# Moving the fourth score wave, the value products and a magnitude within the loop of the first attention

## The reference

```python
# x: 8 batches x 100 tokens x 256, context: 8 x 361 x 192, 16 heads of 16
q = (x @ Wq + bq).reshape(B, N, 16, 16)
k = (y @ Wk + bk).reshape(B, M, 16, 16)
v = (y @ Wv + bv).reshape(B, M, 16, 16)
attn = softmax(einsum('bnhd,bmhd->bhnm', q, k) / 4)
out = einsum('bhnm,bmhd->bnhd', attn, v).reshape(B, N, 256)
h = relu(out @ W1 + b1);  result = h @ W2 + b2
# beside it, for the second block: two linear layers of the context with
# ternary weights; the scale of each weight comes from
w_scale = maximum(mean(abs(W)), 1e-5)     # W_f1 is 128 x 4096 on the chip
```

## Time and profile before

| | |
|---|---|
| median of 3 runs | 597.01 us (595.83 to 597.95) |
| profiled execution, own time | 595.76 us |
| its span | 593.6 us |
| PE busy | 578.7 us, 97% of the span |
| DVE busy | 385.5 us, 65% |
| ACT busy | 219.2 us, 37% |
| POOL busy | 137.3 us, 23% |
| chain that ended last, by engine | PE 76%, DVE 17%, ACT 3%, DMA 2% |

### The profile page before, as it was taken

How to read it: one execution, slowest core, us unless ns; L and a number is a source line. 1 busy time by engine, 2 the same in 40 slices (tenths; PEclk the granted TensorE clock), 3 DMA queues, 4 the chain that set the end, 5 groups by cost and what they waited for, 6 DMA issues and landing times.

```text
span 593.6 us, 10354 instructions
## 1 busy us (share of the span) xinstructions
PE 578.7 (97%) x3971; PEld 428.8 (72%) x3971; DVE 385.5 (65%) x928; ACT 219.2 (37%) x513; POOL 137.3 (23%) x172
## 2 busy tenths in 40 slices
PE   9999999999999999999999989999999999999997
PEld 7766344544456767999999748767787888887587
DVE  1996767587884765222222579886999879775454
ACT  3554665566673374222222376585200010001000
POOL 0053200114004402222222000004355555440000
PEclk9999999999999999999999999999999999999999
DMA  8920000002001562999998100610733662320001
GB/s 187 314 106 1 19 1 1 14 26 57 2 1 28 202 216 79 314 334 368 330 328 294 64 2 0 208 43 1 255 128 105 210 219 89 107 81 0 1 28 29
DMA packets 25695, 71.07 MB, mean 120 GB/s; under 512 B 5271, under 2 KB 13063, under 8 KB 21815
## 3 DMA queue, kind: packets, MB, share of 16 engines
q1 hardware_dynamic: 21910, 58.15, 30.1%
q0 software_dynamic: 3744, 12.38, 6.3%
HBM read 65.02 MB, written 5.49 MB: 119 GB/s over the span
## 4 chain that ended last, share of the span: by engine, by line
PE 76%; DVE 17%; ACT 3%; DMA 2%; issue 1%; SPq 0%; POOL 0%; DVEq 0%; POOLq 0%
PE bank L2193 10%; PE bank L1999 8%; PE bank L2012 8%; PE bank L1821 8%; PE bank L2271 7%; PE bank L1666 7%; PE bank L2181 6%; PE bank L1795 5%; PE bank L1839 3%; PE bank L1764 2%; PE bank L1827 2%; DMA x<-in_x 2%; DVE stats L586 1%; PE bank L1645 1%; DVE nmax L1063 1%
## 5 line engine op out<-in xcount | busy, mean ns | idle before, releaser
L2193 PEld LDWEIGHTS bank<-region,kvT 128*128 128x128 f32 x448 | 77.0, 190 | 9.9 <-issue 0.9
L2193 PE MATMUL bank<-region,kvT 128*128 128x200 f32 x448 | 81.1, 333 | 0.8 <-DVE region L1180 0.8
L761 DVE TENSOR_REDUCE nmax<-bank 100x2 f32<-100x722 f32 x64 | 55.2, 905 | 24.8 <-PE bank L1795 24.4
L1999 PEld LDWEIGHTS bank<-stage,region 128*128 128x128 f32 x448 | 52.1, 192 | 1.4 <-issue 0.8
L1999 PE MATMUL bank<-stage,region 128*128 128x128 f32 x448 | 52.4, 275 | 0.5 <-ACT stage L1490 0.5
L2012 PE MATMUL bank<-region,stage 128*128 128x256 f32 x224 | 50.7, 379 | 0.0
L2181 PE MATMUL bank<-region,kvT 128*128 128x400 f32 x128 | 48.5, 502 | 0.6 <-DVE region L1187 0.6
L2012 PEld LDWEIGHTS bank<-region,stage 128*128 128x128 f32 x224 | 41.5, 190 | 5.1
L2271 PE MATMUL bank<-region,kvt 128*128 128x200 f32 (+1 forms) x192 | 44.5, 389 | 0.3 <-DVE region L1247 0.3
L977 DVE TENSOR_SCALAR stage<-bank,stage 128x128 f32<-128x128 f32 x56 | 15.8, 344 | 44.2 <-PE bank L1999 44.2
L1513 ACT ACTIVATE stage<-bank,stage 128x128 f32<-128x128 f32 x56 | 16.0, 368 | 66.3 <-PE bank L1999 46.6
(11 more groups left out here) (360 smaller groups left out, 1094.9 us busy)
## 6 DMA issues: line engine op xcount, KB each, us to landing
region<-in_e_w SPq DMA_DIRECT2D x28, 1024.0 KB, 4.9
kvT<-in_p_qkv SPq DMA_DIRECT2D x32, 384.0 KB, 3.1
stage<-w_dram POOLq DMA_DIRECT2D x2, 1600.0 KB, 13.6
stage<-in_t_f SPq DMA_DIRECT2D x1, 2048.0 KB, 15.0
kvt<-in_p_o SPq DMA_DIRECT2D x1, 2048.0 KB, 8.7
stage<-in_e_b SPq DMA_DIRECT2D x14, 128.0 KB, 6.1
region<-in_ctxT SPq DMA_DIRECT2D x3, 541.5 KB, 14.0
stage<-w_dram POOLq DMA_DIRECT2D x3, 400.0 KB, 5.3
```

The source lines that it names most:

```text
L761: dve.tensor_reduce(nmax[:, b % 2, at_h:at_h + 9:8], banks[0:N, bank:bank + 2, 0:M], AX.X, ALU.max, negate=True)\
L1999: ins = pe.matmul(psum[2 * u + m // 4][:, (m % 4) * P:(m % 4 + 1) * P], e_w1[u][:, k, m * P:(m + 1) * P], xsT[u][:, k, :], start=k == 0, s ...
L2193: return pe.matmul(bank, left, right, start=e == 0 and i % 2 == 0, stop=e == E1 - 1 and i in (1, 3, 5, 6))
```

## The change

Four things move, all within this loop, and nothing is added to or taken from the work:

- Wave 3 of batch n + 1 moves from ahead of the fifth pair (u = 8) to ahead of the sixth (u = 10).
- The values, which stood as quarters 0 and 1 ahead of the fourth pair and 2 and 3 ahead of the sixth, now stand in three places: 0 and 1 ahead of the fourth pair, 2 ahead of the fifth, 3 ahead of the sixth.
- At u = 6, values still stand before wave 2. At u = 10, wave 3 now stands before values 3.
- ACT's pieces of the magnitude move from behind the fifth and eleventh exponential (u = 4 and 10) to behind the sixth and tenth (u = 5 and 9).

```diff
@@ scalar engine, inside the loop over u
-                        if n in (3, 4) and u in (4, 10):
-                            f1_magnitude(2 * (n - 3) + u // 6)
+                        if n in (3, 4) and u in (5, 9):
+                            f1_magnitude(2 * (n - 3) + u // 9)
@@ tensor engine, inside the loop over u
-                    if u in (6, 10) and 1 <= n <= B:
-                        values(n - 1, u // 2 - 3)
-                        values(n - 1, u // 2 - 2)
-                    if u in (6, 8) and n + 1 < B:
-                        score_wave(n + 1, u // 2 - 1)
+                    if u == 10 and n + 1 < B:
+                        score_wave(n + 1, 3)
+                    if u in (6, 8, 10) and 1 <= n <= B:
+                        for w in {6: (0, 1), 8: (2,), 10: (3,)}[u]:
+                            values(n - 1, w)
+                    if u == 6 and n + 1 < B:
+                        score_wave(n + 1, 2)
```

## The result

The changed kernel takes 602.38 us (600.65 to 604.99, 6 runs) against 597.08 us (595.83 to 597.95, 6 runs): the ratio is 1.0096, with a 95% interval of 1.0075 to 1.0117. I forecast 597.5, between 595.0 and 599.3, and held no change for the likeliest. The profiled execution took 601.19 us with a span of 599.2, against 595.76 and 593.6.

What follows compares the result with a forecast made beforehand. PE bounds the loop, with DVE's latency from wave 3 to `turn_maxima` deciding in five of seven iterations. Terms 1.33 - 0.05 + 0.23 - 1.92 + 0.37 + 0.57 gave +0.53 us, a median of 597.5, range 595.0 to 599.3.

Steps and rivals of the forecast that it cites:

- The paces of PE: PE's loop: a pair with its chain unit takes 1.45 us, a pair alone 1.04, a free wave 0.87.
- the added value group: Values on PE: one more group costs 0.12 us beside its products, so a quarter alone takes 0.645.
- the holds of wave 3: Wave 3 on PE: DVE holds it 0.42 us in iterations 1, 2, 6 and 0.80 in 3, 4; these go.
- Iteration 0, +1.33: Iteration 0: the following `turn_maxima` moves from 73.42 to 74.75, all DVE's; no hold to gain.
- The 4.37 from wave 3 to `turn_maxima`: Iterations 0, 1, 2, 5, 6: `turn_maxima` starts no earlier than 4.37 us after wave 3's start.
- the split keeps its length wherever it stands: DVE: first maximum to split's end takes 3.42 us with two chain maxima, 2.69 without, as before the change.
- Iterations 3 and 4, -1.92: Iterations 3 and 4: PE leads, -0.68 us each from wave 3's hold, -0.28 for each late magnitude piece.
- the magnitude's -0.56: ACT, `turn_maxima` to wave 1: -0.28 us for each of two late magnitude pieces moved.
- the cover: Iterations 3 and 4: ACT's bank 7 copy, behind the moved magnitude, just comes in time; else a tenth or two, twice.
- The end of the loop, -0.26: Behind iteration 6: the first pair, held by ACT's copy of the turned maxima, gives back about 0.26 of 0.29 us.
- Rival 2: Iterations 4 to 6: DVE, also rescaling, doesn't catch up at waves 1 and 2; +2.4 us, median 599.4, chance 0.11.
- the three things by which I said I'd be wrong: L1808 showing no wait on L774, waves 1 or 2 longer than 0.87, or L1851 waiting for ACT over 0.1.

Runs made afterwards that it cites:

- POOL's product late: The changed kernel with POOL's query-spreading product (L488) started later, beside DVE's maxima of wave 0 (wave 1 for b = 6): 597.67 us, ratio 1.0003.
- the two iterations alone and POOL late: The kernel before with ACT's half, L488 on POOL later, and PE's half in iterations 3 and 4 only: 595.49 us, ratio 0.9970.
- ACT's half stood alone: The kernel before with only the magnitude's pieces moved, to u = 5 and 9: 596.69 us, ratio 0.9987.
- the kernel before with POOL late: The kernel before with only POOL's product L488 started later: 598.50 us, ratio 1.0014.
- the version of four iterations: The kernel before with ACT's half, L488 later, DVE's split ahead of the chain maxima, PE's half in iterations 1 to 4: 596.00 us, ratio 0.9976.
- iteration 0 alone: The kernel before with PE's half of the change in iteration 0 only: 601.27 us, ratio 1.0054.

## Why the prediction was wrong

It forecast +0.53 us and the time rose by 5.3. By its steps:

- **The paces of PE, the added value group, the holds of wave 3: right.** Wave 3 starts at 70.38 in iteration 0, as worked out, and a quarter of the values takes 87.56 to 88.21, or 0.65.
- **Iteration 0, +1.33: right in kind.** It is +1.44 with POOL's product late and +1.79 with it beside the split. That PE itself would be there at 73.43 was wrong: wave 0 is held for 0.42. It changed nothing, since DVE came last.
- **The 4.37 from wave 3 to `turn_maxima`: 0.1 short, by itself.** In iterations 5 and 6, which no POOL product touches, it is 154.55 - 150.08 = 4.47 and 170.57 - 166.10 = 4.47. PE starts 0.14 after the split's end, where I had taken 0.05 from a half wave.
- **That the split keeps its length wherever it stands: wrong, and this is the step that failed.** I took 3.42 and 2.69 from rows in which POOL was idle, wrote down for each moved PE step what DVE and ACT do behind it, and never asked what PE's last product of a batch releases on POOL. Seen from the start of POOL's product the move put the split 1.5 to 2.7 us later, under a product of 1.52 us that used to start 0.05 to 1.7 us behind its end. Of the 4.43 us of the loop 4.26 are this (133.73 - 129.47). In iterations 3 and 4, for which I had claimed that PE leads, the forecast gain became a loss: from `turn_maxima` 3 to 5 PE takes 29.43 against 28.94 before.
- **Iterations 3 and 4, -1.92: right once POOL is away.** With the two iterations alone and POOL late, the loop ends 2.05 sooner. Of the parts, the magnitude's -0.56 is there in full: from `turn_maxima` to wave 1 iterations 4 and 5 take 3.00 and 3.81 with POOL late (2.99 and 3.80 in the changed kernel) against 3.28 and 4.09 before. L1851 waits for no copy in either, so the cover held; the late copy that took 0.28 back came only where ACT's half stood alone.
- **The end of the loop, -0.26: one term too small and one missing.** It is -1.0 (from `turn_maxima` 7 to the end 21.47 in place of 22.46). Half of it, 0.49, is gone by the fourth pair of iteration 7 (6.90 after `turn_maxima` in place of 7.39): before, ACT came into this iteration late and held its first pairs. The other half, 0.51, lies between the fourth pair and the sixth (3.77 in place of 4.28). There is no wave in iteration 7, but its values move too, and my sum stopped at iteration 6. Before, the fifth pair waited there for ACT, and now the quarter of the values ahead of it fills that wait:

```profile
174.23 0.99 PE L1821 MATMUL bank<-xT,kvt 64*119 64x400 f32 x3 [0.17 <-ACT kvT L1469]
```

- **The sum, +0.53, with POOL late: near, and in part by luck.** That run ends at +0.17. At `turn_maxima` 7 it stands at +1.17 where my terms gave +0.80, and the end of the loop gives 0.7 more back than I had.
- **The rivals.** Rival 2 had the right sign and said that DVE would not catch up, but put it on the rescaling at waves 1 and 2, where nothing was held. The mechanism that decided wasn't among them. Nor did any of the three things by which I said I'd be wrong come up: what contradicted me was a gap in iterations 3 and 4, where I had said there is none.

0.9 us of the 5.3 are not the loop's. At full clock the kernel before has a median of 596.6 (57 of the 75 executions beside which the variants were timed) and the changed one 601.2 (5 of 12), which is 4.6. The rest is that seven of 12 executions of the changed kernel, and 18 of those 75 of before, were at a lower mean clock. The gaps ahead of `turn_maxima` aren't shown to be the cause: the kernel before with POOL late has no such gaps and had six of 12, and the version of four iterations, without them too, seven of 12. In the profiles that caught a low stretch it lay before 60 us in three, at 75 to 79 in one and at 400 to 450 in two. The one at 75 us did follow straight on a gap of 1.30, but in the two profiles of the changed kernel, and in that of iteration 0 alone, the same gap was followed by full clock. What brings it on stays open. So does why these two profiles, at full clock, are 1.2 us longer behind the loop than the one of before (407.2 and 407.3 us against 406.0).

## What to carry to other kernels

When a step is moved, look up on every engine what runs at its new place, also on those that it neither waits for nor is waited for by: DVE and POOL hold each other without a semaphore between them. An instruction that is longer than its kind while the timeline of the other engine shows one that ends at the same moment is the sign. And before PE's waits are moved, see which engine has the shortest chain at the new place: putting four small operations ahead of two that `turn_maxima` doesn't wait for was worth 2.8 us here, with POOL's product late, where the change itself, with that product late, was worth nothing (+0.17). In the kernel before, where `turn_maxima` waited for nothing, it was not tried.

## What the runs showed of the hardware

A cast of 100x16 on DVE, 0.20 us by itself, took up to 1.55 us under a product of two SBUF operands on POOL (1.52 us), and ended 0.04 to 0.06 after it. A memset on POOL held the cast too, but not a difference of two SBUF operands on DVE (0.19 us). Maxima from PSUM (0.90) and from SBUF (0.5) were never held. The hold is by whole instructions and by who comes first: an operation that started 0.15 us ahead of POOL's kept its 0.18 us. The reverse is seen once in each profile, though no edit tested it: POOL's product of 1.52 us took 2.8 when it started within a DVE operation on SBUF. In the kernel before, DVE's ended at 59.95 and POOL's at 61.33:

```profile
57.60 2.35 DVE L726 SCALAR_TENSOR_TENSOR tern<-region,wabs,tern 128x2048 bf16<-128x2048 f32 x1
```

```profile
58.55 2.78 POOL L488 TENSOR_TENSOR w_a<-xn,consts 128x800 f32<-128x800 f32 x1 [9.69 <-PE bank L1666]
```
